# One decoder layer on one core: state scans joined in pairs, with the carry added in PSUM, and expert biases written into PSUM by ScalarE

## The reference

```python
# Mamba: 512 channels, 16 states for each
dt = softplus(proj[..., -1:] * W_dt[:, 0] + b_dt)
def step(h, inp):
    dt_t, Bt, Ct, xt = inp
    dA = exp(dt_t[..., None] * A)
    h = dA * h + (xt * dt_t)[..., None] * Bt[:, None, :]
    return h, einsum('bdn,bn->bd', h, Ct)
# expert e of four, weighted by a softmax over the best two scores
h = relu(layernorm(xf @ w1 + b1, g1, be1))
out_e = layernorm(h @ w2 + b2, g2, be2)
```

## Time and profile before

| | us |
|---|---|
| median of 3 runs | 1890.12 |
| range of the runs | 1887.43 to 1891.87 |
| the profiled execution: its time | 1887.57 |
| its span (first to last instruction) | 1885.8 |

### The profile page before, as it was taken

The page is one execution under the profiler, slowest core; times in us unless marked ns, Lnnn a source line. Parts: engine busy times, 40 slices in busy tenths (PEclk is TensorE's granted clock), DMA queues, the critical chain, the costliest instruction groups (busy, mean ns, idle before and its releaser), DMA issues. The chain is left out here.

```text
span 1885.8 us, 26716 instructions
## 1 busy us (share of the span) xinstructions
PE 1511.5 (80%) x8112; PEld 1073.2 (57%) x8112; DVE 1483.3 (79%) x2801; ACT 1043.4 (55%) x2290; POOL 907.7 (48%) x717
## 2 busy tenths in 40 slices
PE   4777788777877787778866679988998899889890
PEld 3666667665766666666755344546455645564470
DVE  1899999999999999999999353386458645864478
ACT  3667866786668766877664215226622662266151
POOL 0677767776777777777776100003600360036005
PEclk9888899988988898889876779999999999999895
DMA  3311110111011101111010300100020001000000
GB/s 129 118 47 51 63 37 27 63 64 52 12 63 62 63 3 62 62 63 34 24 57 12 124 1 1 49 1 1 1 71 1 2 1 45 1 1 1 23 0 23
DMA packets 38437, 71.24 MB, mean 38 GB/s; under 512 B 3697, under 2 KB 31954, under 8 KB 33970
## 3 DMA queue, kind: packets, MB, share of 16 engines
q1 hardware_dynamic: 38290, 69.45, 11.0%
HBM read 60.79 MB, written 8.65 MB: 37 GB/s over the span
## 5 line engine op out<-in xcount | busy, mean ns | idle before, releaser
L605 POOL TENSOR_TENSOR state_c<-state,c_bc 128x1024 f32<-128x1024 f32 x256 | 603.3, 2361 | 232.9 <-DVE state L668 220.1
L668 DVE TENSOR_TENSOR_SCAN state<-decay,carry,bu_ps 128x256 f32<-128x256 f32 x768 | 528.6, 730 | 0.0
L485 ACT ACTIVATE decay<-dt_sb,negA 128x256 f32<-128x256 f32 x1024 | 433.8, 498 | 3.1 <-issue 3.1
L1277 POOL TENSOR_TENSOR big<-big,g_sb 128x1024 f32<-128x1024 f32 x29 | 77.8, 2681 | 628.5 <-ACT big L1179 626.9
L653 DVE TENSOR_TENSOR bu_ps<-u_sb,b_ps 128x512 f32<-128x512 f32 x512 | 346.1, 676 | 43.4 <-POOL u_sb L546 37.2
L350 PE MATMUL y_ps<-ident_sb,state_c 128*128 128x128 f32 x2048 | 306.6, 299 | 20.8 <-DVE yg L636 12.9
L350 PEld LDWEIGHTS y_ps<-ident_sb,state_c 128*128 128x128 f32 x2048 | 265.7, 156 | 52.1 <-POOL state_c L605 25.0
L271 PE MATMUL w_ps<-xT_sb,w_conv 128*128 128x256 f32 (+1 forms) x1024 | 235.9, 384 | 12.9 <-DVE w_conv L706 11.9
L271 PEld LDWEIGHTS w_ps<-xT_sb,w_conv 128*128 128x128 f32 x1024 | 191.8, 192 | 39.0 <-DVE w_conv L706 11.9
L668 DVE TENSOR_TENSOR_SCAN state<-decay,bu_ps 128x256 f32<-128x256 f32 x256 | 160.6, 669 | 0.0
L334 PE MATMUL b_ps<-parts,sel_bc_sb 96*128 96x256 bf16 x256 | 77.0, 302 | 102.7 <-DVE bu_ps L653 92.9
(11 more groups left out here) (165 smaller groups left out, 2388.6 us busy)
## 6 DMA issues: line engine op xcount, KB each, us to landing
c_bc<-c_scratch SPq DMA_DIRECT2D x32, 1024.0 KB, 6.3
res<-in_x SPq DMA_DIRECT2D x16, 256.0 KB, 2.8
x_scratch<-res SPq DMA_DIRECT2D x16, 256.0 KB, 7.3
stage<-x_scratch SPq DMA_DIRECT2D x4, 1024.0 KB, 7.9
xa<-x_scratch SPq DMA_DIRECT2D x4, 1024.0 KB, 5.9
out_x<-acc SPq DMA_DIRECT2D x4, 1024.0 KB, 4.5
xT_sb<-in_xT SPq DMA_DIRECT2D x12, 259.0 KB, 3.0
w_sb<-in_w SPq DMA_DIRECT2D x2, 1024.0 KB, 13.5
```

Source lines behind the costliest of these rows:

```text
L485: nc.scalar.activation(decay[:, n % RING, j, :], dt_sb[:, i[1] % 2, j, :], ACT.Exp, scale=negA[:, j * NS + n:j * NS + n + 1]).then_inc(s_d ...
L605: nc.gpsimd.tensor_tensor(state_c[:, n % RING, :, :], state[:, n % RING, :, :], c_bc[:, q, n, :].unsqueeze(1).to_broadcast([P, CT, TC]), A ...
L668: nc.vector.tensor_tensor_scan(state[:, n % RING, j, :], decay[:, n % RING, j, :], bu_ps[m % 3][:, e * TC:(e + 1) * TC], carry[:, n, j:j + ...
```

## The change

**Scans in pairs.** A pair of channel tiles is now one scan over 512 columns. Column 0 of every `decay` tile is set to zero once and ACT writes only columns 1 to 255, so the recurrence starts afresh at each tile. What the carry would have brought, `dA_0 * carry`, is computed by POOL (`first_arg`, `injections`) and ACT (`first_decay`), and DVE adds it to column 0 of both tiles in PSUM (`add_carry`, 128x2) between the scans. `s_bu` now counts four for each step, so that `b_row` waits for the `add_carry` as well; in chunks with no carry `make_bu` counts two.

**Expert biases.** The bias matmuls go. ACT copies the biases (128x1024, from SBUF) into both banks of a tile ahead of the products (`preset`), which all accumulate. The three-part split on DVE goes; the biases come by one broadcast transfer instead. `xT` now shares its buffer with `x1T`.

```diff
@@ Mamba, PE: b_row @@
-                pe.wait_ge(s_bu, at(i, 2 * NS, 2 * n + 2))
+                pe.wait_ge(s_bu, at(i, 4 * NS, 4 * n + 4))
@@ Mamba, ACT @@
+            def first_decay(k):
+                act.wait_ge(s_arg, at(k, 1, 1))
+                nc.scalar.activation(first_dA[:, k[1] % 2, :, :], first_dA[:, k[1] % 2, :, :], ACT.Exp).then_inc(s_dA, 1)
-                    nc.scalar.activation(decay[:, n % RING, j, :], dt_sb[:, i[1] % 2, j, :], ACT.Exp,
+                    nc.scalar.activation(decay[:, n % RING, j, 1:], dt_sb[:, i[1] % 2, j, 1:], ACT.Exp,
+                if prepare:
+                    work.append((15, lambda: first_decay(k)))
@@ Mamba, POOL @@
+            def first_arg(k):
+                q = k[1] % 2
+                if is_first(k):
+                    pool.wait_ge(s_par, 2)
+                pool.wait_ge(s_dt, at(k, 1, 1))
+                nc.gpsimd.tensor_tensor(first_dA[:, q, :, :], dt_sb[:, q, :, 0].unsqueeze(1).to_broadcast([P, NS, CT]),
+                                        negA[:, :].rearrange("p (j n) -> p n j", n=NS), ALU.mult).then_inc(s_arg, 1)
+
+            def injections(k, first, last):
+                if k[1] % CPB == 0:
+                    pool.sem_inc(s_inj, 1)
+                    return
+                if first == 0:
+                    pool.wait_ge(s_dA, at(k, 1, 1))
+                pool.wait_ge(s_carry, at(k, NS, last - NS))
+                nc.gpsimd.tensor_tensor(inject[:, first:last, :], first_dA[:, k[1] % 2, first:last, :],
+                                        carry[:, first:last, :], ALU.mult).then_inc(s_inj, 1)
...
-                             (12, lambda: make_u(k))]
+                             (11, lambda: first_arg(k)), (12, lambda: make_u(k)),
+                             (13, lambda: injections(k, 0, NS - RING))]
+                work.append((4, lambda: injections(i, NS - RING, NS)))
@@ Mamba, DVE @@
+            def add_carry(i, n, h):
+
+                m = 2 * n + h
+                if i[1] % CPB == 0:
+                    return
+                if m == 0:
+                    dve.wait_ge(s_inj, at(i, 2, 1))
+                elif m == 2 * (NS - RING):
+                    dve.wait_ge(s_inj, at(i, 2, 2))
+                dve.wait_ge(s_bu, at(i, 4 * NS, 8 + 2 * m + 1))
+                begin = bu_ps[m % 3][:, :].rearrange("p (j n) -> p j n", j=2)[:, :, 0]
+                nc.vector.tensor_tensor(begin, begin, inject[:, n, 2 * h:2 * h + 2], ALU.add).then_inc(s_bu, 1)
...
-                for e in range(2):
-                    j = 2 * h + e
-                    dve.wait_ge(s_decay, at(i, NS * CT, n * CT + j + 1))
-                    nc.vector.tensor_tensor_scan(state[:, n % RING, j, :], decay[:, n % RING, j, :],
-                                                 bu_ps[m % 3][:, e * TC:(e + 1) * TC],
-                                                 carry[:, n, j:j + 1] if c else 0.0, ALU.mult, ALU.add).then_inc(s_scan, 1)
+                dve.wait_ge(s_bu, at(i, 4 * NS, 8 + 2 * m + 2))
+                dve.wait_ge(s_decay, at(i, NS * CT, n * CT + 2 * h + 2))
+                pair = slice(2 * h, 2 * h + 2)
+                nc.vector.tensor_tensor_scan(state[:, n % RING, pair, :].rearrange("p j n -> p (j n)"),
+                                             decay[:, n % RING, pair, :].rearrange("p j n -> p (j n)"),
+                                             bu_ps[m % 3][:, :], 0.0, ALU.mult, ALU.add).then_inc(s_scan, 1)
...
                 scans(i, n, 0)
+                add_carry(i, n, 1)
...
                 scans(i, n, 1)
+                if n + 1 < NS:
+                    add_carry(i, n + 1, 0)
+                elif prepare:
+                    add_carry(shift(i, 1), 0, 0)
@@ experts, PE, first layer (the second likewise) @@
-                    if t >= 2:
-                        pe.wait_ge(s_l1c, b * TT + t - 1)
+                    pe.wait_ge(s_pre, b * 2 * TT + t + 1)
                     for h in range(2):
                         dst = ps[:, 2 * (t % 2) + h, :]
-                        nc.tensor.matmul(dst, ones3_sb[:, :], brow[:, h * HALF:(h + 1) * HALF], start=True, stop=False)
@@ experts, ACT @@
+                def preset(t):
+
+                    if t < 2:
+                        act.wait_ge(s_ytc, b * TRB + TRB)
+                    elif t < TT + 2:
+                        act.wait_ge(s_l1c, b * TT + t - 1)
+                    else:
+                        act.wait_ge(s_l2c, b * TT + t - TT - 1)
+                    nc.scalar.activation(ps[:, 2 * (t % 2):2 * (t % 2) + 2, :],
+                                         biases[:, t // TT, :].rearrange("p (a n) -> p a n", a=2),
+                                         ACT.Copy).then_inc(s_pre, 1)
...
                 copy_transposed(b, xT, 0, s_yt, s_ytc)
+                preset(0)
+                preset(1)
...
+                    preset(t + 2)
...
+                        if t + 2 < TT:
+                            preset(TT + t + 2)
```

More of the change, by code:

```diff
@@ L82, in mamba_block @@
         carry = sb("carry", [P, NS, CT])
+        first_dA = sb("first_dA", [P, 2, NS, CT])
+        inject = sb("inject", [P, NS, CT])
         rest = sb("rest", [PARTS * BC, TC])
@@ L145, in mamba_block @@
         s_carry = sem("s_carry")
+        s_arg = sem("s_arg")
+        s_dA = sem("s_dA")
+        s_inj = sem("s_inj")
+        s_zero = sem("s_zero")
         s_sc = sem("s_sc")
@@ L522, in _ @@
             next_lead(first)
+            first_decay(first)
             act.wait_ge(s_par, 2)
@@ L622, in _ @@
             make_u(first)
+            first_arg(first)
+            injections(first, 0, NS - RING)
             turns(pool, turn)
@@ L650, in make_bu @@
                     dve.wait_ge(s_b, at(i, NS, n + 1))
-                dve.wait_ge(s_scan, at(i, NS * CT, RING * CT + 2 * (m - (1 if m < 2 else 2))))
+                dve.wait_ge(s_scan, at(i, 2 * NS, RING * 2 + m - (1 if m < 2 else 2)))
                 nc.vector.tensor_tensor(bu_ps[m % 3][:, :].rearrange("p (j n) -> p j n", j=2),
@@ L741, in attn_ffn_block @@
         bqk_sb, bv_sb, swap_sb, gw_sb, gb_sb = (w[n] for n in ("bqk", "bv", "swap", "gw", "gb"))
-        lnp_sb, ones3_sb = (w[n] for n in ("lnp", "ones3"))
+        lnp_sb = w["lnp"]
         g2_sb = sb("g2_sb", [P, E * DM])
@@ L745, in attn_ffn_block @@
         before_sb = sb("before_sb", [P, E * E])
-        brow = sb("brow", [3 * BLK, 2 * E * DM], BF16)
+        biases = sb("biases", [P, 2, E * DM])
         xa = sb("xa", [P, TT, DM])
@@ L877, in _ @@
             sp.dma_start(be2_sb[:, :], be2.partition_broadcast(P)).then_inc(s_const, 16)
+            sp.dma_start(biases[:, :, :].rearrange("p a n -> p (a n)"), bias_rows.partition_broadcast(P)).then_inc(s_const, 16)
             sp.dma_start(before_sb[:, :], before.partition_broadcast(P)).then_inc(s_const, 16)
@@ L905, in transposes @@
                     for i in range(TG):
-                        last = nc.tensor.transpose(ps[:, bank + u, i * P:(i + 1) * P],
-                                                   src[:, half * TG + i, k * P:(k + 1) * P], ident_sb[:, :])
+                        last = nc.tensor.matmul(ps[:, bank + u, i * P:(i + 1) * P],
+                                                src[:, half * TG + i, k * P:(k + 1) * P], ident_sb[:, :],
+                                                start=i == 0, stop=True, is_transpose=True, skip_group_check=True)
                     last.then_inc(done, 1)
@@ L1113, in turn @@
                         t = n * TG + i
-                        if t >= 2:
-                            pe.wait_ge(s_l2c, b * TT + t - 1)
-                        else:
-                            pe.wait_ge(s_l1c, b * TT + TT)
+                        pe.wait_ge(s_pre, b * 2 * TT + (TT + t + 1))
                         for e in range(E):
@@ L1121, in turn @@
                                 pe.wait_ge(s_hc, b * NT * E * KT + E * KT * n + KT * (e + 1))
-                            if e % 2 == 0:
-                                nc.tensor.matmul(ps[:, 2 * (t % 2) + e // 2, :], ones3_sb[:, :],
-                                                 brow[:, E * DM + e * DM:E * DM + (e + 2) * DM],
-                                                 start=True, stop=False, skip_group_check=True)
                             for k in range(KT):
@@ L1576, in _ @@
             keys_values(0, 0)
-            dve.wait_ge(s_brow, 16)
-            row = big[0:3 * BLK, 1, 0:2, :].rearrange("p a n -> p (a n)")
-            left = big[0:3 * BLK, 1, 2:4, :].rearrange("p a n -> p (a n)")
-            nc.vector.tensor_copy(brow[:, :], row).then_inc(s_split, 1)
-            dve.wait_ge(s_split, 1)
-            nc.vector.tensor_tensor(left, row, brow[:, :], ALU.subtract).then_inc(s_split, 1)
-            dve.wait_ge(s_split, 2)
-            for q in (1, 2):
-                nc.vector.tensor_copy(brow[BLK * q:BLK * q + BLK, :], left[BLK * q:BLK * q + BLK, :]).then_inc(s_split, 1)
-            dve.wait_ge(s_split, 4)
```

(13 more changed lines are left out.)

36 lines of the change are left out of this document (15 added, 21 removed).

## The result

The changed kernel took 1874.24 us (median of 4 runs, 1872.89 to 1881.87), the kernel before 1890.99 (1887.43 to 1892.52). The ratio is 0.9921, with a 95% interval from 0.9896 to 0.9946: 17 us less by the medians, 15 by the ratio. The forecast was 1856.5, 34 less, with 1872 as the upper end of its range. The direction was right and the size was not.

What follows compares the result with a forecast made beforehand. It took DVE to bound the Mamba block and PE most of the second block. From 1887.57 us, 13 less for scans and 19 for biases gave 1855.6, plus about 1: 1856.5, range 1846 to 1868.

Steps and rivals of the forecast that it cites:

- VectorE's 42 us: Scan loop: VectorE's own saving over 384 pairs with carry and 128 without, if nothing else came last.
- The pair, 1.78 us: VectorE, chunk with carry: make_bu 0.58, one 512-column scan 1.11, add 0.09; 1.78 us in place of 1.87.
- Rival B: Scan loop: the add costs its full 0.17 us, scans gain 0 or lose 4; 1871 us, chance 0.14.
- the sum of 15 us: VectorE's own saving if the add cost 159 ns, by the Trainium skill page's fixed term.
- The chain of u: Chunks with carry: b_row 1.2 us later and first_arg 0.3 make u late; VectorE waits 1.1 us a chunk.
- the second new wait: Start of 12 chunks with carry: VectorE's add_carry waits 0.87 us more for POOL's inject.
- Part 1: Scan loop: scans in pairs, 13 us less in sum, between 7 and 22.
- D: Scan loop: PE's half clock moves up to step 4, 49 us over 11 chunks; slower, 1905 us, chance 0.04.
- Part 2: Experts: 128 bias matmuls save 28 us, less 5.3 and 3.7; 19 us less, between 14 and 24.
- The relu: Experts: the sixth tile's preset on ACT delays the relu PE waits for; 4 x 0.92 = 3.7 us lost.
- Rival A: Scan loop: VectorE's gain comes through, 30 to 42 us in place of 13; 1833 us, chance 0.14.
- Rival C: Experts: PE waits before each tile for ACT's two copies, the biases' gain is gone; 1875 us, chance 0.08.

Runs made afterwards that it cites:

- row_free: Changed kernel, but TensorE's b row of a step waits for make_bu alone, not for the carry's add behind it: 1863.50 us.
- u_early: row_free with GpSimd making the next chunk's u at place 11, ahead of first_arg, and the first injection at place 12 instead of 13: 1849.12 us.
- scans_only: Kernel before with only the scan loop's changes, experts unchanged: 1884.84 us, ratio 0.9979 to the kernel before.
- act_order: Changed kernel with two second-layer presets later on ScalarE: tile 5's behind the second half's second relu, tile 6's behind the guess: 1865.60 us.
- no_bias: Changed kernel without presets, leaving out expert biases b1 and b2; each preset becomes a bare semaphore count: 1865.38 us.
- early_order: Changed kernel with the edits of u_early and act_order together: 1841.34 us, ratio 0.9732 to the kernel before.

## Why the prediction was right in direction and wrong in size

- **What bounds the kernel**: right. VectorE paced the loop, and what came last behind it was what the forecast named: row_free and u_early, which only take waits away, gave 25 us. The forecast had 29 of VectorE's 42 us turn into waits. (In the earlier trace rows the nines begin at the third slice, not the second; nothing hangs on it.)
- **The pair, 1.78 us**: right to 0.01, with errors that cancel: the scan's distance is 1.13 (forecast 1.11), make_bu's 0.59 to 0.60 (0.58) and the add's 0.05 (0.09). Rival B falls with it, and so does the sum of 15 us for an add that takes its whole 0.16: it is recorded with 0.15 us, but moves the next start by 0.05.
- **The chain of u and the second new wait**: the mechanism was right and the sizes near, 1.35 and 0.67 us for 1.1 and 0.87, TensorE 1.04 later at its step 3 for 1.2. Undisturbed chunks came to 61.2 to 61.3 for 60.9, 0.3 to 0.4 more in each of eleven. Not seen was that the new chunk's own b row is nearly as late as u: behind the start-up the profile names u at 6 chunk starts and the b row at the 9 others.
- **Part 1, 13 less**: too large. It is 4 by the medians of scans_only. By the loop's length it is 7.5 to 8.1 in scans_only, act_order and no_bias, and 2.3 and 0.6 in the two traces of the changed kernel. Two steps are missing from the sum. The first is the jump of the loop over sequences, put at nothing. Chunks 6 and 10 follow it; VectorE's idle time behind it grew from 1.2 to 1.3 us to 2.7 to 3.2, 3 in all, and TensorE's clock fell there, so that they took 64.4 us in scans_only. The second is the step that I called D, taken for all chunks or none ("if the fall moves up to step 4", 49 us, 0.04). It came in part, in 4 and 5 chunks of the two traces of the changed kernel, in one of scans_only and in none of act_order and no_bias, at 2 us each. I had argued that TensorE's total idle time falls, but what stood ahead of each fall was one wait that had got longer. The clock fell at this place before the change too: it is 0.77 over steps 3 and 4 of chunks 3, 6 and 9, against 1.00 in chunk 5. There the chain of u had slack, and chunks 3 and 9 took 62.3 to 62.4 us, hardly more than the 61.9 to 62.2 of most others. In the changed kernel that slack is used up.
- **Part 2, 19 less**: the step that failed most; 7 by the medians, 6.1 in the trace. The bias matmuls were worth nearly what they took in the second layer (TensorE from start to start 13.0 us less, of a priced 14.1), but in the first only 4.5 of 14.1, where 8.8 had been forecast. The first layer of the first three sequences was to gain half of 10.6 us and gained 3.6; the last sequence gained 0.9 of 3.5. Two things took it. TensorE waits longer for VectorE, and not in tiles 4 to 7 alone: in the last sequence, where the forecast had no such bound, it is through 3.2 us sooner and then waits 2.30 for `big`. And behind the score maxima's matmuls the products themselves became slower. A group of four with the next one's start, before and after:

```profile
1219.13 1.88 PE L1085 MATMUL ps<-w_sb,xT_sb 128*128 128x512 f32 x4
1220.94 0.81 PE L963 MATMUL ps<-kT,qT 32*128 32x154 f32 x16
```

```profile
1222.31 1.98 PE L1135 MATMUL ps<-w_sb,x1T_sb 128*128 128x512 f32 x4
1224.23 0.81 PE L1015 MATMUL ps<-kT,qT 32*128 32x154 f32 x16
```

  That is 1.92 us for 1.81, half of what the bias matmul took, in 36 of the 64 groups, some 4 us in all. It is the same in no_bias, so it isn't the presets.

  The relu was priced at 3.7: TensorE does wait 1.09 more at that row, but the second layer as a whole is only 0.5 to 0.6 shorter in each sequence of act_order, so some 2.3 was its net cost. "Elsewhere ACT has over 2 us to spare for a tile" is where the sum broke. By its own numbers it is 1.6 us (twice 1.7 less twice 0.92). As a statement on TensorE's waits it held; but the guess is on ScalarE's queue too, with VectorE and the next attention behind it, and I had not looked at who waits for that. The scores of the next sequences became 4.6 us longer than before, 3.4 of them through this, and the wait at the end 2.0 (5.6 against 3.6).
- **Rival A** (30 to 42 for the scans) did not happen, but is what early_order shows once the waits are gone: its loop takes 949.9 us, 31 less than before. **Rival C** (TensorE waits for presets) is refuted: in the trace no instruction of any engine waits for one of the 64, and in act_order 9 us come back with every preset still there.
- **The forecast's range and chances** have two slips. Parts of 7 to 22 and 14 to 24 give 1843 to 1868, not 1846 to 1868. And 0.94 for a faster kernel is 0.01 too much beside 0.04 for D and 0.03 for what lies above.

Both profiled executions of the changed kernel were some 7 us over its other runs, of which there is no trace. With the loop of act_order and no_bias (973.1 us) and a start at 53.2 us, as before, in place of 978.8 and 56.0, the first would have taken 1881.9 - 5.7 - 2.8 = 1873.4 us. This is an estimate from these traces; it lies where the other runs do.

What stays open: the clock's fall behind equal waits in one execution and not in another, and why the scores of the next sequences are 2.0 us longer than before even in no_bias.

## What to carry to other kernels

When an operation gets a follower on the same engine, ask of each waiting engine whether it needs the follower or only the first one: the wait on the wrong one of the two cost more here than the scans had gained. When work is added to an engine with time to spare, look at each small operation that it already carries and at who waits for it, since idle time on average hides nothing at the one place where a chain runs through that engine. And when a bound engine gets faster, the feeders' order has to be set anew: the move of u that was worth nothing before was, with that of the injection, worth 14 us after.
